# Attention scores from two float32r parts, two heads in the two halves of TensorE's rows

## The reference, cut to what matters

```
q = _split_heads(Q @ Wq.T + bq)          # Q is the normalised x, 16 heads of 16
k = _split_heads(K @ Wk.T + bk)          # K is the context
scores = jnp.einsum('bhqd,bhkd->bhqk', q, k) * scale
attn = jax.nn.softmax(scores, axis=-1)
ctx = jnp.einsum('bhqk,bhkd->bhqd', attn, v)
```

## Time and profile before

| | |
|---|---|
| median of three executions | 468.47 us (466.15 to 469.18) |
| span of the profiled execution | 466.8 us; its own time is not recorded apart from the span |
| busy: TensorE, VectorE, ScalarE, GpSimd | 453.6, 331.8, 252.6, 154.4 us |
| attention steps with maxima | 2.84 us each |

### The profile page before, as it was taken

The page is one execution under the profiler, slowest core; times in us unless marked ns, Lnnn a source line. Parts: engine busy times, 40 slices in busy tenths (PEclk is TensorE's granted clock), DMA queues, the critical chain, the costliest instruction groups (busy, mean ns, idle before and its releaser), DMA issues.

```text
span 466.8 us, 8100 instructions
## 1 busy us (share of the span) xinstructions
PE 453.6 (97%) x2310; PEld 215.8 (46%) x2310; DVE 331.8 (71%) x841; ACT 252.6 (54%) x540; POOL 154.4 (33%) x209
## 2 busy tenths in 40 slices
PE   8999999999999999999999989889999999999997
PEld 8664432222222222222465634565555555555745
DVE  1988898888888888888578766354565656532674
ACT  2664477777777777777565111023666766631110
POOL 5493488111212121212132766600323332332000
PEclk9999999999999999999999999979999999999999
DMA  8669762335353535353548522311322222312921
GB/s 261 223 181 251 157 204 58 86 83 97 90 98 94 98 94 97 95 92 102 167 135 264 211 91 81 110 48 46 93 84 88 85 88 83 90 49 60 377 101 47
DMA packets 54140, 56.71 MB, mean 121 GB/s; under 512 B 13456, under 2 KB 44560, under 8 KB 54096
## 3 DMA queue, kind: packets, MB, share of 16 engines
q1 hardware_dynamic: 47504, 43.82, 34.1%
q0 software_dynamic: 4960, 10.53, 7.4%
q10 hardware_dynamic: 1632, 1.84, 1.2%
HBM read 36.35 MB, written 17.72 MB: 116 GB/s over the span
## 4 chain that ended last, share of the span: by engine, by line
PE 90%; DVE 4%; issue 2%; DMA 1%; SPq 1%; another core or an unknown queue 1%; POOL 1%; ACT 1%; DVEq 0%; POOLq 0%
PE PS L1395 13%; PE PS L1305 13%; PE PS L1523 12%; PE PS L1567 11%; PE PS L1677 9%; PE PS L1580 6%; PE PS L1696 5%; PE PS L1357 4%; PE PS L1672 3%; PE PS L1442 3%; PE PS L1691 2%; PE PS L1651 2%; DVE nmax L842 2%; PE PS L1335 2%; PE PS L1659 2%
## 5 line engine op out<-in xcount | busy, mean ns | idle before, releaser
L842 DVE TENSOR_REDUCE nmax<-PS 128x1 f32<-128x512 f32 x256 | 159.4, 683 | 21.4 <-PE PS L1305 21.4
L730 ACT ACTIVATE R<-PS 128x512 f32<-128x512 f32 x256 | 134.1, 601 | 42.0 <-PE PS L1523 41.7
L1305 PE MATMUL PS<-R 96*128 96x512 bf16 x256 | 96.1, 382 | 1.2 <-DMA R<-k_parts 1.0
L1523 PE MATMUL PS<-R 98*128 98x512 bf16 x256 | 86.2, 380 | 0.3 <-DVE R L860 0.3
L1395 PE MATMUL PS<-R 128*32 128x512 f32 x512 | 68.2, 604 | 0.0
L621 POOL DMA_INDIRECT token_y<-R,dest x34 | 32.6, 960 | 93.4 <-DVE R L1184 92.0
L1305 PEld LDWEIGHTS PS<-R 96*128 96x128 bf16 x256 | 24.8, 97 | 69.7 <-DVE nmax L842 51.1
L1677 PE MATMUL PS<-R 128*128 x100 | 47.3, 595 | 0.2 <-ACT R L798 0.2
L745 ACT ACTIVATE R<-PS 128x512 f32<-128x512 f32 x16 | 9.6, 597 | 68.7 <-PE PS L1567 52.1
L600 POOL DMA_DIRECT2D CH<-R x56 | 27.4, 496 | 54.4 <-ACT R L718 54.4
L1523 PEld LDWEIGHTS PS<-R 98*128 98x128 bf16 x256 | 24.8, 97 | 38.6 <-ACT R L730 22.6
(11 more groups left out here) (177 smaller groups left out, 598.4 us busy)
## 6 DMA issues: line engine op xcount, KB each, us to landing
R<-q_parts SPq DMA_DIRECT2D x96, 64.0 KB, 3.1
R<-k_parts SPq DMA_DIRECT2D x96, 64.0 KB, 3.1
R<-in_fc_w_dram SPq DMA_DIRECT2D x16, 256.0 KB
R<-token_y SPq DMA_DIRECT2D x4, 1024.0 KB, 9.0
R<-slot_x SPq DMA_DIRECT2D x25, 129.0 KB
k_parts<-R SPq DMA_DIRECT2D x8, 384.0 KB, 3.3
q_parts<-R SPq DMA_DIRECT2D x8, 384.0 KB, 3.5
fc<-in_fc_w_dram SPq DMA_DIRECT2D x16, 128.0 KB
```

Source lines behind the costliest of these rows:

```text
L730: nc.scalar.activation(PT[:, kt, j, :], PS[:, (G * (TB * i + kt) + j) % 3, :], ACT.Exp).then_inc(exp_done, 1)
L842: nc.vector.tensor_reduce(nmax[:, i % 2, j * TB + qt:j * TB + qt + 1], PS[:, smax_bank(n), :], AX.X, ALU.max, negate=True).then_inc(max_re ...
L1305: mm(PS[:, smax_bank(n), :], QS[g][0:KS, j, qt * P:(qt + 1) * P], KST[g][0:KS, j, :], start=True, stop=True).then_inc(smax_done, 1)
L1523: mm(PS[:, n % 3, :], KST[g][0:KM, j, kt * P:(kt + 1) * P], QS[g][0:KM, j, :], start=True, stop=True).then_inc(st_done, 1)
```

## The change

The three bfloat16 parts become two parts in float32r, a float32 that is rounded when it is written. Three products of parts (high x high, low x high, high x low) take the place of six, so a head needs 48 rows instead of 96, and 50 instead of 98 with the maxima. Two heads of a group then fit, one in rows 0 to 63 and one in rows 64 to 127: `QS` and `KST` hold `h` (0 or 1) along the free dimension and `r` (0 or 1) as the half. `second_part` and `third_part` go; VectorE writes the low part itself. Group loads stay 12 of 64 KB, stores grow from 384 to 512 KB. `load_max` writes two partitions of 4 KB instead of one. The ones of the last rows are set by GpSimd at the start, for whole `KST`.

The order in a step becomes S0, M0, S1, M1, S2, (turned maxima), `values`, M2, S3, M3, and `max_tile` pairs heads and query tiles so that the halves are, in this order, 0, 1, 1, 0, 0, then 1, 1, 0.

```diff
-    TERMS = 6
-    Q_PART = [0, 1, 2, 0, 1, 0]
-    K_PART = [0, 0, 0, 1, 1, 2]
+    TERMS = 3
+    Q_PART = [0, 1, 0]
+    K_PART = [0, 0, 1]
+    UNIT = 2 * TERMS
+    HALF = P // 2
...
+        def max_tile(n):
+
+            i, m = divmod(n, G * TB)
+            h, m = divmod(m, 2 * TB)
+            qt, r = m // 2, 1 - m % 2
+            return i, (h, r, qt), 2 * TB * r + TB * h + qt
...
-                for t in terms:
-                    sp.dma_start(QS[g][t * DK:(t + 1) * DK, :, :],
-                                 q_scr[b, Q_PART[t], rows, :].rearrange("(h d) n -> d h n", h=G)).then_inc(ld_group[g], 16)
...
+                for piece in pieces:
+                    t, r = divmod(piece, 2)
+                    at = slice(HALF * r + t * DK, HALF * r + (t + 1) * DK)
+                    sp.dma_start(QS[g][at, :, :].bitcast(F32),
+                                 q_scr[b, Q_PART[t], rows, :].rearrange("(h r d) n -> r d h n", r=2, d=DK)[r])\
+                      .then_inc(ld_group[g], 16)
...
-            def second_part(b, j):
-                act.wait_ge(rest_ready, 4 * b + j + 1)
-                nc.scalar.copy(QP[:, j, 1, :], REST[:, j, :]).then_inc(q2_ready, 1)
...
-                nc.vector.scalar_tensor_tensor(out=REST[:, j, :], in0=PS[:, qk_bank(b, j), :],
+                dve.wait_ge(high_ready, 4 * b + j + 1)
+                nc.vector.scalar_tensor_tensor(out=QP[:, j, 1, :], in0=PS[:, qk_bank(b, j), :],
...
-                mm(PS[:, smax_bank(n), :], QS[g][0:KS, j, qt * P:(qt + 1) * P], KST[g][0:KS, j, :],
+                mm(PS[:, smax_bank(n), :], QS[g][at, h, qt * P:(qt + 1) * P], KST[g][at, h, :],
                    start=True, stop=True).then_inc(smax_done, 1)
...
-                    mm(PS[:, n % 3, :], KST[g][0:KM, j, kt * P:(kt + 1) * P], QS[g][0:KM, j, :],
+                    h, r = divmod(j, 2)
+                    at = slice(HALF * r, HALF * r + KM)
+                    mm(PS[:, n % 3, :], KST[g][at, h, kt * P:(kt + 1) * P], QS[g][at, h, :],
                        start=True, stop=True).then_inc(st_done, 1)
...
                     scores(kt, 0)
+                    mx[0]()
                     scores(kt, 1)
-                    mx[0]()
+                    mx[1]()
                     scores(kt, 2)
-                    mx[1]()
                     if kt == 2 and i + 1 < GROUPS:
                         max_transpose(i + 1)
```

More of the change, by code:

```diff
@@ L10 @@
 F32 = mybir.dt.float32
-BF16 = mybir.dt.bfloat16
+F32R = mybir.dt.float32r
 U32 = mybir.dt.uint32
@@ L52, in flamingo_layer @@
     EPS = 1e-5
-    q_scr = nc.dram_tensor("q_parts", (B, 3, D, S), BF16, kind="Internal").ap()
-    k_scr = nc.dram_tensor("k_parts", (B, 3, D, S), BF16, kind="Internal").ap()
+    q_scr = nc.dram_tensor("q_parts", (B, 2, D, S), F32, kind="Internal").ap()
+    k_scr = nc.dram_tensor("k_parts", (B, 2, D, S), F32, kind="Internal").ap()
     TURNED = GROUPS - 2
@@ L101, in flamingo_layer @@
         minus_half = sb("minus_half", [P, NT])
+        with nc.sbuf_tensor("QK", [P, 8192], F32R) as QK:
+            pass
         R1 = sb("R1", [P, 8192])
@@ L114, in flamingo_layer @@
         CT = R2[:, 4096:6144].rearrange("p (s c n) -> p s c n", s=2, c=DC)
[L115 to L120, removed]
+        QP = R3[:, 4096:8192].rearrange("p (j a n) -> p j a n", j=4, a=2)
+        QS = [QK[:, 1024 * g:1024 * (g + 1)].rearrange("p (h n) -> p h n", h=2) for g in range(NG)]
+        KST = [QK[:, 4096 + 1024 * g:4096 + 1024 * (g + 1)].rearrange("p (h n) -> p h n", h=2) for g in range(NG)]
         PT = R2[:, :].rearrange("p (k h n) -> p k h n", k=TB, h=G)
@@ L204, in flamingo_layer @@
         wq_scaled = sem("wq_scaled")
-        q1_ready, q2_ready, q3_ready = (sem(n) for n in ("q1_ready", "q2_ready", "q3_ready"))
-        rest_ready = sem("rest_ready")
+        high_ready, low_ready = sem("high_ready"), sem("low_ready")
         qp_out = sems("qp_out", 4)
@@ L344, in parts_stored, with load_group @@
                     sp.wait_ge(qp_out[j], 16 * (b + 1))
-            def load_group(i, terms=range(TERMS)):
+            def load_group(i, pieces=range(UNIT)):
                 b, g = divmod(i, NG)
@@ L349, in load_group @@
                     sp.wait_ge(st_done, G * TB * (i - NG + 1))
+                else:
+                    sp.wait_ge(kones, g + 1)
                 rows = slice(g * G * DK, (g + 1) * G * DK)
-                for t in terms:
-                    sp.dma_start(QS[g][t * DK:(t + 1) * DK, :, :],
-                                 q_scr[b, Q_PART[t], rows, :].rearrange("(h d) n -> d h n", h=G)).then_inc(ld_group[g], 16)
-                    sp.dma_start(KST[g][t * DK:(t + 1) * DK, :, :],
-                                 k_scr[b, K_PART[t], rows, :].rearrange("(h d) n -> d h n", h=G)).then_inc(ld_group[g], 16)
+                for piece in pieces:
[4 more added lines that the diff above has]
+                      .then_inc(ld_group[g], 16)
+                    sp.dma_start(KST[g][at, :, :].bitcast(F32),
+                                 k_scr[b, K_PART[t], rows, :].rearrange("(h r d) n -> r d h n", r=2, d=DK)[r])\
+                      .then_inc(ld_group[g], 16)
             def load_max(i):
@@ L359, in load_max @@
                     sp.wait_ge(s, i + 1)
-                    sp.dma_start(QS[i % NG][KS + part:KS + part + 1, :, :].rearrange("p h n -> p (h n)"),
+                    sp.dma_start(QS[i % NG][KS + part:P:HALF, :, :].bitcast(F32).rearrange("p h n -> p (h n)"),
                                  mparts[:, i % 2, part, :]).then_inc(m_in[i % 2], 16)
@@ L403, in _ @@
                 if 0 < i and i + 3 < GROUPS:
-                    load_group(i + 3, range(0, TERMS - 2))
+                    load_group(i + 3, range(0, UNIT - 2))
                 if i + 1 < GROUPS:
@@ L407, in _ @@
                 if 0 < i and i + 3 < GROUPS:
-                    load_group(i + 3, range(TERMS - 2, TERMS))
+                    load_group(i + 3, range(UNIT - 2, UNIT))
                 if 0 <= i - 1 < TURNED:
@@ L529, in rstd_first @@
                 nc.gpsimd.tensor_tensor(rstd[:, sl], var_eps[:, sl], minus_half[:, sl], ALU.pow).then_inc(ln_rstd, 1)
-            def third_part(b, j):
-                pool.wait_ge(q2_ready, 4 * b + j + 1)
-                nc.gpsimd.tensor_tensor(QP[:, j, 2, :], REST[:, j, :], QP[:, j, 1, :], ALU.subtract).then_inc(q3_ready, 1)
             rstd_first(0)
             rstd_first(1)
[L537 to L554, removed]
+            for g in range(NG):
+                nc.gpsimd.memset(KST[g][:, :, :].bitcast(F32), 1.0).then_inc(kones, 1)
+                if g == 1:
+                    rstd_first(2)
+            rstd_first(3)
+            pool.wait_ge(kones, NG)
+            pool.wait_ge(w_in["small"], 64)
+            for c in range(DC):
+                nc.gpsimd.tensor_scalar(bv_wide[:, c, :], ones[:, :], bv_col[:, c:c + 1], None, ALU.mult).then_inc(bv_ready, 1)
+            pool.wait_ge(bv_ready, DC)
+            pool.wait_ge(scaled, 3)
+            nc.gpsimd.tensor_scalar(tg_bo[:, :], bo_row[:, :], tg[:, 0:1], None, ALU.mult).then_inc(bo_scaled, 1)
+            pool.wait_ge(bo_scaled, 1)
             def rstd_second(b):
@@ L835, in one_max @@
             def one_max(n):
-                s, qt = divmod(n, TB)
-                i, j = divmod(s, G)
+                i, _, at = max_tile(n)
                 dve.wait_ge(smax_done, n + 1)
@@ L1285, in scores_for_max @@
             def scores_for_max(n):
-                s, qt = divmod(n, TB)
-                i, j = divmod(s, G)
+                i, (h, r, qt), _ = max_tile(n)
                 b, g = divmod(i, NG)
-                if j == 0 and qt == 0:
-                    pe.wait_ge(ld_group[g], 16 * 2 * TERMS * (b + 1))
+                if n % (G * TB) == 0:
+                    pe.wait_ge(ld_group[g], 16 * 2 * UNIT * (b + 1))
+                at = slice(HALF * r, HALF * r + KS)
                 if n == 0:
@@ L1298, in scores_for_max @@
                 if n == 14:
-                    pe.wait_ge(rest_ready, 4 * (B - 1))
+                    pe.wait_ge(low_ready, 4 * (B - 1))
                 if n == 15:
```

27 lines of the change are left out of this document (10 added, 17 removed).

## The result

| | before | after |
|---|---|---|
| median of five executions | 468.47 us (465.85 to 469.18) | 479.45 us |
| ratio, 95% interval | | 1.025 (1.020 to 1.030) |
| profiled execution: time, span | span 466.8 us | 482.42, 480.7 us |

The change makes the kernel 2.5% slower; 461 was forecast. The other executions of the changed kernel lie between 477.28 and 482.42; one took 514.03 at a mean granted clock of 0.893, and the ratio leaves it out.

A forecast was written before the change was run, and what follows sets the result against it. TensorE, never idle in the attention stage with VectorE 10% behind, was taken as the bound. Gains of 6.2 us (14 group periods), 0.3 (group 0) and 1.0 (before attention) sum to 7.5, from 468.5 to 461.0; range 453 to 470.

The forecast's parts named there:

- the weight load at no cost: Attention step: float32r loads of 141 or 190 ns lie under another product and cost nothing, up to 0.03 us a product.
- The early maxima products: Pairs in different halves between float32 products: 0.22 us saved, two switches added, in sum nothing.
- Group 0: First attention group, its steps paced by a VectorE behind from the projections: 0.3 us gained.
- The clock: A fall in the attention stage would make the sum wrong; no chance given, as gaps stay under half a microsecond.
- the loop through M2's reduction: Attention step: M1 waits for M2's reduction, at least 1.16 us after M2; this sets the step at 2.69 us.
- the exp's loop: Attention step: S2 of the next step waits for S3's exp, at least 1.09 us after S3; step 2.62 us.
- the first loads' wait: TensorE's 0.98 us wait for the first group's loads goes, as a rounding and a subtraction before them go.
- the turned maxima's DMAs: Between groups: rows land 3.9 us after the transpose, next group's S0 comes at 4.2; hidden, 0.3 to spare.
- No overlap: Rival: halves do not run side by side, eight products take 8 x 0.22 us as before; 467 us, chance 0.12.
- two passes: Rival: each float32r product takes the 0.43 us of a float32 record; 493 us, chance 0.10.
- dearer switches: Rival: each switch into or out of halves costs 0.16 us instead of 0.09; 466 us, chance 0.10.
- Weight loads uncovered: Rival: uncovered weight loads together with no overlap of halves, 0.25 us a product; 481 us, chance 0.06.

The follow-up runs named there:

- Experiment 2: Changed kernel with its two parts in bfloat16 instead of float32r, halves, order and waits unchanged, scores less exact: 467.25 us, ratio 0.995.
- experiment 11: Kernel before with maxima products over 48 of their 96 rows, so that TensorE changes its tiling more often in a step: 507.7 us (one execution).
- experiment 6: Changed kernel with ten maxima products (last two early ones, eight of group 0's first two steps) made twice: 478.81 us, ratio 1.024.
- experiment 5: Changed kernel with VectorE reducing only 256 of 512 columns for each maximum: 471.3 us (one execution).
- experiment 10: Changed kernel, float32r halves, with the order of the kernel before (S0, S1, M0, S2, M1): 491.2 us (one execution).
- experiment 3: Changed kernel with S2 ahead of M1 and the maxima products' halves swapped, so every pair lies in different halves: 470.1 us, ratio 1.002.
- experiment 7: Changed kernel, float32r, with every pair in different halves and ten early maxima products made twice: 467.58 us, ratio 1.0004.

## Why the prediction was wrong

**The step that failed is the weight load at no cost.** The forecast took the longer load as free "when it lies under another product", and priced only the case of too many loads at once, at 0.03 a product. Nor does that price follow from its own figures: two loads of 190 ns in the 0.22 of one product would leave 0.16 over. The runs show neither, since loads start 0.11 apart; a covered float32r product takes 0.24 for 0.22. What the forecast did not ask is where in its own loop no product lies over the load. There are two such places: behind `values`, and where M1's load has waited for its bank. Each costs 0.11 to 0.12 (1.28 for 1.16 from M2 to M1, 0.33 for 0.22 from M1 to S2). Both are in the loop that the forecast had found to set the step, so 2.69 became 2.93 and 11.06 became 11.94: 0.9 us in each of 13 to 14 groups, 12 of the 18 us between forecast and result (461.0 and 479.45). Experiment 2 takes the longer load away and gives 2.70 and 11.09.

The row was there: the two kinds of 4-byte load take 141 and 190 ns for bfloat16's 97. I called either harmless. Float32r loads take 188, like those of full float32 (experiment 2 has 94 for bfloat16). The Trainium skill's rule that the fast load is not for FP32 ("TensorE: Matmul & The Clock Gate", "Weight-path perf modes") was weighed and set aside for the same reason. The trace agrees with it: 188 ns for 94. That difference, where it lies uncovered, decided the case.

**The early maxima products** were put down at nothing, 0.22 saved for two changes of tiling. Here the maxima products lie alone between float32 products in whole rows: four records of the latter take 1.91 us behind a pair in the halves for 1.72 before, also with bfloat16 parts. 0.1 of that is the change (experiment 11); the rest is put down to the float32 load of the next product, now uncovered, which no run shows by itself. Nor did the pair save anything with float32r: 0.42 us (36.24 to 36.66) for the 0.44 of before, 0.32 with bfloat16. As an estimate, some dozen times 0.2 us is 2.4 us, more than the wait of 0.98 that did go: the first transpose came 1.4 later instead of 1.0 earlier.

**Group 0** was forecast at 0.3 us less than the 13.2 of before, from the first transpose to the second. Without the fall of the clock it took 14.5 (experiment 6), 1.6 over the forecast. With shorter reductions it took 12.6 (experiment 5), so the length of the reductions counts there too; the rest of it was not traced.

**The clock** was given no chance because gaps in the steady steps stay short. That held for the steady steps. But in the first steps of the attention stage, where VectorE is behind, the halves make TensorE's share of the work smaller, and in the profiles its clock fell right behind them. This was a rival the forecast should have had, with the window of 290 to 310 us before its eyes. It cost 3 us in the profile. The execution of 479.45 did not have these ten us, so they are no part of the 18 us.

**What held:** one pass for a float32r product; full overlap of halves; the loop through M2's reduction, with the exp's loop close behind (experiments 5 and 10); 0.1 for a change of tiling; the first loads' wait; the turned maxima's DMAs, for which no product waited in the steady groups of the changed kernel (in experiments 3 and 7, with a shorter step, one did). "No overlap", "two passes" and dearer switches did not come about. "Weight loads uncovered" was a rival, but only without overlap, and its 481 was near for the wrong reason. The remaining 1 us or so between the last transpose and the end, without the fall, was not traced. One of the signs failed with the step: VectorE was busy for 86% of 88 to 160 us, not over 93%. And the lower end of the range leaves out the 1.3 us gained elsewhere; with VectorE's floor and these it would be 451.

## What to carry to other kernels

- A load or a wait is free only where something covers it at that point of the loop that sets the time. Walk that loop instruction by instruction, and ask at each whether the one before it in the queue was held up by a wait or by a change of tiling: there the load stands alone.
- When products become shorter, the dependence that was just covered becomes the step, and the order in which the last few instructions wait is worth more than the products saved. Here the same products, ordered and laid into the halves in three ways, took 11.2, 11.9 or 12.5 us a group.
- Float32r saves rows against three bfloat16 parts, at one pass a product, but its weights load as slowly as float32. With 128 columns of weights and waits in the queue, two bfloat16 parts were 2.8% faster than the kernel before, at less exact scores, where float32r at its best was level.

## What the runs showed of the hardware that was not expected

- Products in different halves of the rows don't keep the order of the queue. M3 stands behind S3 in it, yet starts with M2 (103.50, two records), 0.34 before S3, which comes behind M2 in its own half. So "each engine takes its instructions in order", as said of the kernel before, does not hold for the starts of TensorE's products here.
- A float32r load takes 188 ns by its record and the next starts 0.11 later; bfloat16 94 ns. Covered, a float32r product follows another in its half by 0.24 us, a bfloat16 one by 0.22.
- A change between half and whole rows costs 0.10 us each way.
- TensorE's clock fell from 2.4 to 1.2 GHz 64 to 66 us after the start in all six profiles of kernels with halves and full reductions that kept those ten products single. It did not in the three with the products made twice, nor with shorter reductions. Between 60 and 64 us TensorE was busy for 1.35 to 2 us of each 2 in the six. But the kernel before, with 1.54 of 2 at 60 to 62 us, had no fall, so this share alone does not tell the two apart.
